# Four graph layers on one core: where GpSimd waits between the row gathers of the last attention layer

## The chip, the core and the metric

The kernel runs on one core of a Trainium2 chip. The metric is device microseconds of a plain (not profiled) execution. Three such executions of the kernel before took 5525.43, 5527.91 and 5542.02 us; the median is 5527.91 us. Engines are named PE (TensorE), PEld (its weight loads), DVE (VectorE), ACT (ScalarE), POOL (GpSimd) and SP (the queue that issues plain DMAs).

## The reference

A node table x of 3125 x 64 goes through four residual graph layers over the same 100,000 edges, sorted by destination: a GAT layer, a two-step SAGE layer, a layer that multiplies gathered rows by edge attributes, and a softmax attention with 8 heads, where the change is. Cut to what matters:

```
h = maximum(layernorm(x), 0)
src, dst = edges plus one self loop per node
z = (h @ W_att).reshape(n, 8, 64)
e = leaky_relu(a_src[src] + a_dst[dst], 0.2)         # a score per edge and head
e = exp(e - segment_max(e, dst)[dst])
alpha = e / (segment_sum(e, dst)[dst] + 1e-16)
out = segment_sum(alpha[:, :, None] * z[src], dst)   # then mean over heads, layer norm, feed-forward
```

## The kernel before

The four layers run one after the other. The changed loop is in `attend3`, the attention of the last layer (tiles with the prefix `l3_` in the program, `l_` in profile rows). What it does:

- The edges are cut into 782 tiles of 128 (`TILES`). For each tile POOL issues one indirect DMA, which gathers 128 rows of 73 floats (64 features, a one, 8 source scores) from `table3` into one of 320 places of the ring `rows` (`RING3`), at L1740. This is the loop `for t in range(TILES)` of the `gpsimd` block.
- 64 tiles are a part (`PART`), 13 parts in all (`NP`). A part's scores are made together: PE turns the gathered scores around (`turn_far`, L1898) once all its tiles have landed; DVE adds, takes running maxima and chains them over the tiles (`score`, L1759 to L1789, `join`, `settle`); ACT takes the exponentials (L1969).
- The sums go in 981 steps, each a pair of a tile and a window of 16 nodes, 4 steps to a group, 246 groups. For a group ACT copies the weights (`step_att`, L1981), DVE builds `hot` (L1845), PE multiplies (`sums`, L1934, two matmul records a step) and counts `sums_ready` up by one, DVE adds into `acc` (L1855). Places and windows are read at run time into registers (L194, TENSOR_LOAD, and FUSED_REGOPS, which work them out).
- Part p+1 is scored in the middle of part p: after the fifth group of a part (`SCORED` = 4) come `turn_far` and `score`, after the eighth `join`, after the eleventh `settle`. A part has 16 groups, the last part the rest.

The order of every engine is written out by hand; nothing is scheduled at run time, and the engines meet only at semaphores. POOL waits at two places in its loop. One is `landed` (L1739): before a tile it waits until the DMAs of the eight gathers just issued (a batch, `U` = 8) have landed. The other is `sums_ready` (L1737): before tiles t to t+7 go into the ring it waits until so many groups of sums are done that the old tiles in these places are certainly used up. The count that it waits for is (t + 7 - 320 + 199) // 4 + 1, that is (t - 114) // 4 + 1, where 199 is the number of windows less one. `RING3` (320), `REST` (2), `U` (8) and `PART` (64) are constants at the top.

Of the kernel before, what the change touches and what calls it, by code (L numbers as in the profile page):

```python
# [32 lines left out]
U = 8  # L33
# [23 lines left out]
REST = 2  # L57
# [20 lines left out]
PART = 64  # L78
NP = -(-TILES // PART)
RING3 = 320  # L80
# [1540 lines left out]
def part_tiles(p):  # L1621
    return min(PART, TILES - PART * p)


def attend3(nc, m):
# [6 lines left out]
    with ExitStack() as stack:  # L1632
# [41 lines left out]
        def landed(b):  # L1674

            return rows_in[b % RING], base[b % RING] + 16 * U * (b // RING) + 16 * min(U, TILES - U * b)
# [47 lines left out]
        @block.gpsimd  # L1724
        def _(pool):
            nc.gpsimd.memset(key_i[2][:, :], -1).then_inc(keys_blank, 1)
            def tile_firsts(p, landed):
                n = part_tiles(p)
                pool.indirect_dma_start(tile_first[0:n, p, :], None, m.node_values[:, :],
                                        bass.IndirectOffsetOnAxis(ap=m.first_tile[0:n, p:p + 1], axis=0)).then_inc(landed, 16)  # L1730
            tile_firsts(0, first_in)
            for t in range(TILES):
                if t == PART:
                    for p in range(1, NP):
                        tile_firsts(p, firsts_in)
                if t >= RING3 and t % 8 == 0:
                    pool.wait_ge(sums_ready, (t + 7 - RING3 + NW - 1) // STEPS + 1)  # L1737
                if t and t % (REST * U) == 0:
                    pool.wait_ge(*landed(t // U - 1))  # L1739
                pool.indirect_dma_start(rows[:, t % RING3, :], None, m.table3[:, :],  # L1740
                                        bass.IndirectOffsetOnAxis(ap=m.tile_src[:, t:t + 1], axis=0)
                                        ).then_inc(rows_in[t // U % RING], 16)
            pool.wait_ge(top_written, 16 * NP)
            for c in range(2 * J):
                pool.indirect_dma_start(found[:, c // J, c % J, :], None, m.reference[:, :],
                                        bass.IndirectOffsetOnAxis(ap=m.found_index[:, c // J, c % J:c % J + 1], axis=0)
                                        ).then_inc(found_in, 16)

        @block.vector
        def _(dve):  # L1750
# [61 lines left out]
            def settle(p):  # L1812

                n = part_tiles(p)
                N_ = slice(0, n)
                dve.wait_ge(back, p + 1)
                own(v.tensor_copy(first_last[N_, :, :], small_ps[N_, 4 * PART:4 * PART + 2 * H].rearrange("p (a h) -> p a h", a=2)))
                own(v.tensor_copy(ends[:, 0:1], ends[:, 2 * n:2 * n + 1]))
                if p:
                    _, values = nc.values_load_multi_w_load_instructions(  # L1820
                        m.start_step[0:1, p - 1:p], engines=[mybir.EngineType.DVE], min_val=0, max_val=KJ - 1,
                        skip_runtime_bounds_check_because="a tile's last step is under KJ - 1")
                    own(v.scalar_tensor_tensor(factor[:, bass.ds(values[0], 1)], small_ps[:, 4 * PART + 2 * H:4 * PART + 2 * H + 1],
                                               m.mask3[:, p:p + 1], m.unmask3[:, p:p + 1], ALU.mult, ALU.add))
                for a, inside in enumerate((in_first, in_last)):
                    own(v.tensor_tensor(near[N_, :, :], over(inside[N_, :].unsqueeze(1), (n, H, TILE)),
                                        over(first_last[N_, a, :].unsqueeze(2), (n, H, TILE)), ALU.add))
                    last = v.tensor_tensor(top[N_, :, :], near[N_, :, :], top[N_, :, :], ALU.max)
                    if a == 0:
                        own(last)  # L1830
                last.then_inc(top_ready, 1)
                dve.wait_ge(top_ready, p + 1)
                v.tensor_tensor(z[N_, :, :], z[N_, :, :], top[N_, :, :], ALU.subtract).then_inc(z_ready, 1)
# [508 lines left out]
```

## Time and profile before

| | |
|---|---|
| Plain executions | 5525.43, 5527.91, 5542.02 us |
| Profiled execution, first to last instruction (span) | 5821.8 us |
| Instructions | 59032 |
| PE, DVE, ACT, POOL busy in the span | 57%, 61%, 38%, 38% |
| Gathers of the third layer (L1143) | 782, 2796.6 to 3932.2 us |
| Gathers of the attention (L1740) | 782, 4076.3 to 5381.2 us |
| Steps of the attention (L1934) | 4206.5 to 5619.2 us |

The profiled execution is one execution recorded by the hardware. Its page gives no other time of it than the span; the span alone is 293.9 us longer than the median of the plain executions. All places in time below are microseconds from the span's start. A row "idle before <- X" says how long the engine stood still before that instruction and what ended the wait; "issue" is time for which no cause is recorded. Where such a cause names a DMA of another stage, the semaphore had been used by that DMA before.

### The profile page before, as it was taken

The page shows a single profiled execution, that of the slowest core. Times are in us where ns is not written, and L with a number is a line of the kernel's source. Part 1 is how long each engine was busy: PE and PEld are TensorE (multiplying, and loading weights), DVE is VectorE, ACT ScalarE, POOL GpSimd, SP SyncE. Part 2 cuts the span into 40 slices and gives each one's busy share as a digit, 9 for nine tenths or more (in the row PEclk, how much of TensorE's full clock was granted, in tenths as well). Part 3 has the DMA queues.
Part 4 walks back from the last instruction along what each step waited for, and adds up shares of the span by engine and source line. Part 5 has one row for each costly group of instructions (what it writes and reads, how often), then busy time and mean ns, then how long its engine had stood idle before and what let it go on. Part 6 is the DMA issues. An engine that isn't in the chain of part 4 may idle for free. (4 is left out here: it accounts for less than half of the span.)

```text
span 5821.8 us, 59032 instructions
## 1 busy us (share of the span) xinstructions
PE 3339.7 (57%) x14332; PEld 2165.0 (37%) x14332; DVE 3534.5 (61%) x6569; ACT 2187.4 (38%) x3989; POOL 2214.4 (38%) x2086
## 2 busy tenths in 40 slices
PE   5666679999999999789034332333000443433565
PEld 3555534444444444456032332333000443333452
DVE  6999989999999999310134332333211664545676
ACT  4999967878788887200000000000000111111210
POOL 0000023333333333000666777772777056666200
PEclk8999989999999999899556555555555555555556
DMA  2555544444444443787321422212111012111011
GB/s 74 163 162 162 162 131 114 119 111 111 119 109 116 116 115 97 155 187 157 57 45 38 92 47 43 50 34 22 35 28 33 9 33 36 31 36 30 5 36 35
DMA packets 546254, 474.35 MB, mean 81 GB/s; under 512 B 185774, under 2 KB 439737, under 8 KB 545086
## 3 DMA queue, kind: packets, MB, share of 16 engines
q1 hardware_dynamic: 493723, 416.13, 28.5%
q0 software_dynamic: 52288, 55.34, 5.9%
q8 instruction: 109, 1.79, 0.1%
q14 instruction: 134, 1.09, 0.1%
HBM read 351.39 MB, written 119.84 MB: 81 GB/s over the span
## 5 line engine op out<-in xcount | busy, mean ns | idle before, releaser
L815 PE MATMUL l_sum_ps<-arena,sums 125*65 125x500 f32 (+1 forms) x2600 | 1144.6, 578 | 9.9 <-ACT arena L776 4.8
L1740 POOL DMA_INDIRECT l_rows<-table,tile_src x782 | 768.9, 983 | 521.1 <-issue 232.6
L1143 POOL DMA_INDIRECT l_rows<-hidden_rows,tile_src x782 | 794.9, 1017 | 341.8 <-issue 231.5
L694 POOL COPY arena<-arena 125x750 f32<-125x750 f32 (+1 forms) x400 | 538.9, 1351 | 894.6 <-PE l_count_ps L804 864.9
L760 ACT ACTIVATE arena<-arena,far_left 125x750 f32<-125x750 f32 (+1 forms) x800 | 713.3, 939 | 285.7 <-DVE arena L713 285.7
L713 DVE SCALAR_TENSOR_TENSOR arena<-arena,far_past 125x750 f32<-125x750 f32 (+1 forms) x800 | 807.1, 1055 | 16.1 <-DMA arena<-score_rows 16.1
L1204 PE MATMUL l_sum_ps<-l_rows,l_hot 128*125 x1612 | 360.1, 414 | 768.6 <-issue 651.9
L724 DVE SCALAR_TENSOR_TENSOR arena<-arena,l_count_ps 125x750 f32<-125x750 f32 (+1 forms) x800 | 739.4, 970 | 100.5 <-ACT arena L765 52.0
L1934 PE MATMUL l_sum_ps<-l_rows,l_hot 128*128 x1962 | 483.6, 424 | 439.3 <-issue 268.9
L1170 DVE TENSOR_TENSOR sums<-sums,l_sum_ps 125x64 f32 x806 | 178.6, 222 | 777.9 <-DMA arena<-counts 485.6
L1204 PEld LDWEIGHTS l_sum_ps<-l_rows,l_hot 128*125 128x125 f32 x1612 | 341.3, 322 | 787.7 <-issue 786.9
L1934 PEld LDWEIGHTS l_sum_ps<-l_rows,l_hot 128*128 128x128 f32 x1962 | 437.8, 327 | 483.9 <-issue 481.3
L1855 DVE SCALAR_TENSOR_TENSOR acc<-acc,l_factor,l_sum_ps 128x65 f32 x981 | 276.4, 282 | 542.4 <-DMA found_index<-found_rows 319.6
L765 ACT ACTIVATE arena<-arena 125x1500 f32<-125x1500 f32 (+1 forms) x400 | 596.1, 1491 | 0.0
L507 PE MATMUL l0tab_count_ps<-l0tab_pair_hot,l0tab_src_hot 125*125 125x325 bf16 x2592 | 427.3, 307 | 224.9 <-issue 199.3
L815 PEld LDWEIGHTS l_sum_ps<-arena,sums 125*65 125x65 f32 x2600 | 353.0, 141 | 541.7 <-issue 541.4
L804 PEld LDWEIGHTS l_count_ps<-ident,arena 125*125 125x125 f32 x2500 | 314.4, 192 | 392.3 <-issue 342.9
L1243 ACT ACTIVATE l_end_dense_sb<-l_end_ps_t 128x500 f32<-128x500 f32 (+1 forms) x7 | 3.7, 542 | 1210.0 <-PE l_end_ps_t L1229 1209.9
L507 PEld LDWEIGHTS l0tab_count_ps<-l0tab_pair_hot,l0tab_src_hot 125*125 125x125 bf16 x2592 | 329.7, 137 | 322.6 <-issue 309.2
L804 PE MATMUL l_count_ps<-ident,arena 125*125 125x125 f32 x2500 | 371.4, 287 | 130.3 <-POOL arena L694 55.2
L471 DVE TENSOR_SCALAR l0tab_pair_hot<-code_iota,fine_pair_code 125x650 bf16<-125x650 f16 x1296 | 418.3, 392 | 1.0 <-PE l0tab_count_ps L507 1.0
L486 ACT ACTIVATE arena<-node_iota,fine_src_code 125x125 f32<-125x125 f32 x1296 | 405.9, 384 | 0.0
(440 smaller groups left out, 3021.8 us busy)
## 6 DMA issues: line engine op xcount, KB each, us to landing
arena<-counts SPq DMA_DIRECT2D x300, 328.1 KB
counts<-arena SPq DMA_DIRECT2D x324, 284.4 KB
arena<-counts SPq DMA_DIRECT2D x17, 2843.8 KB
arena<-counts SPq DMA_DIRECT2D x100, 382.8 KB
l_attr<-edge_attr_in SPq DMA_DIRECT2D x97, 256.0 KB
arena<-score_rows SPq DMA_DIRECT2D x24, 732.4 KB
l_rows<-hidden_rows,tile_src POOLq DMA_INDIRECT x782
l_rows<-table,tile_src POOLq DMA_INDIRECT x782
```

Source lines behind the costliest of these rows:

```text
L507: last = nc.tensor.matmul(self.ps[b][0:P, c, 0:CW // 2], self.src_hot[b][:, t, :], self.pair_hot[b][:, t, c * (CW // 2):(c + 1) * (CW // 2 ...
L694: g.tensor_copy(laid[k % 2][:, 0:n * P].rearrange("p (b v d) -> p b v d", b=n, d=D), raw[k % RAWS][:, 0:n * P].rearrange("p (v b d) -> p b ...
L713: last = v.scalar_tensor_tensor(scores(k)[:, i, :], rows[:, 1, i, :], m.far_past[:, w, h:h + 1], rows[:, 0, i, :], ALU.add, ALU.max)
L724: last = v.scalar_tensor_tensor(here, here, LOWEST, over(count_ps[0:P, c, 0:hi - lo].unsqueeze(1), (P, PAIR, hi - lo)), ALU.max, ALU.mult)
L760: last = nc.scalar.activation(here, here, ACT.Relu, scale=-1.0, bias=m.far_left[:, w, h:h + 1])
L765: nc.scalar.activation(scores(k), scores(k), ACT.Exp, scale=-1.0).then_inc(raised, 1)
L804: last = nc.tensor.transpose(count_ps[0:P, i // per, o:o + P], laid[k % 2][:, i * P:(i + 1) * P], m.ident[0:P, 0:P])
L815: last = nc.tensor.matmul(sum_ps[0:F + 1, c, 0:hi - lo], h_one[:, w, :], z[k % ZS][:, lo:hi], start=(w == 0), stop=(w == W - 1))
L1143: pool.indirect_dma_start(rows[:, b % RING, t, :], None, m.hidden_rows[:, :], bass.IndirectOffsetOnAxis(ap=m.tile_src[:, k:k + 1], axis=0) ...
L1204: last = nc.tensor.matmul(sum_ps[r % 4][0:P, j * F:(j + 1) * F], hot[r % 4][:, j, :], flat[:, bass.ds(place, 1), :].rearrange("p a f -> p ...
L1740: pool.indirect_dma_start(rows[:, t % RING3, :], None, m.table3[:, :], bass.IndirectOffsetOnAxis(ap=m.tile_src[:, t:t + 1], axis=0)).then_ ...
L1934: last = nc.tensor.matmul(sum_ps[g % 4][:, i * (F + 1):(i + 1) * (F + 1)], hot[g % 3][:, i, :, :].rearrange("p h j -> p (h j)"), rows[:, b ...
```

## The change

Both conditions of POOL's loop are set by t, the number of the tile.

```diff
@@ -1733,9 +1733,9 @@
                 if t == PART:
                     for p in range(1, NP):
                         tile_firsts(p, firsts_in)
-                if t >= RING3 and t % 8 == 0:
+                if t >= 2 * PART and t % 8 == 0:
                     pool.wait_ge(sums_ready, (t + 7 - RING3 + NW - 1) // STEPS + 1)
-                if t and t % (REST * U) == 0:
+                if t and t % (U if t >= 2 * PART else REST * U) == 0:
                     pool.wait_ge(*landed(t // U - 1))
```

The wait for sums is made from tile 128 on (before: from tile 320, where it is needed to keep the ring intact). The wait for the last eight gathers is made before each eighth tile from 128 on (before: each sixteenth throughout). Up to tile 127, nothing changes. No other engine's instructions and no transfer is changed.

The first place is POOL's order from tile 112 on. `rows_in11` and the like are the semaphores of `landed` (one of twelve for each batch), `shared24` is `sums_ready`; "x15" is fifteen gathers in a row with no wait. In the program before:

```order
L1740 DMA l3_rows<-table3,tile_src 128x73 [waits rows_in1]
L1740 DMA l3_rows<-table3,tile_src 128x73 x15
L1740 DMA l3_rows<-table3,tile_src 128x73 [waits rows_in3]
L1740 DMA l3_rows<-table3,tile_src 128x73 x15
L1740 DMA l3_rows<-table3,tile_src 128x73 [waits rows_in5]
L1740 DMA l3_rows<-table3,tile_src 128x73 x15
```

The same stretch of POOL's order in the changed program:

```order
L1740 DMA l3_rows<-table3,tile_src 128x73 [waits rows_in1]
L1740 DMA l3_rows<-table3,tile_src 128x73 x15
L1740 DMA l3_rows<-table3,tile_src 128x73 [waits rows_in3,shared24]
L1740 DMA l3_rows<-table3,tile_src 128x73 x7
L1740 DMA l3_rows<-table3,tile_src 128x73 [waits rows_in4,shared24]
L1740 DMA l3_rows<-table3,tile_src 128x73 x7
L1740 DMA l3_rows<-table3,tile_src 128x73 [waits rows_in5,shared24]
L1740 DMA l3_rows<-table3,tile_src 128x73 x7
```

The first two rows (tiles 112 to 127) are the same; from tile 128 on a stop stands before each eighth gather, and each also waits for sums.

The second place is POOL's order from tile 320 on, as a piece of the difference between the two programs (- before, + changed):

```order
 L1740 DMA l3_rows<-table3,tile_src 128x73 [waits rows_in3,shared24]
 L1740 DMA l3_rows<-table3,tile_src 128x73 x7
-L1740 DMA l3_rows<-table3,tile_src 128x73 [waits shared24]
+L1740 DMA l3_rows<-table3,tile_src 128x73 [waits rows_in4,shared24]
 L1740 DMA l3_rows<-table3,tile_src 128x73 x7
 L1740 DMA l3_rows<-table3,tile_src 128x73 [waits rows_in5,shared24]
 L1740 DMA l3_rows<-table3,tile_src 128x73 x7
```

Here the stops stay where they were, each eighth gather; every second one, which waited for sums alone, now waits for the landing too.

## Rows read from the trace of the kernel before

**Rows 1.** The page: span, and POOL's busy tenths in 40 slices.
```profile
span 5821.8 us, 59032 instructions
...
POOL 0000023333333333000666777772777056666200
```

**Rows 2.** Busy us (x instructions) by stretch; last PE clock, DMA share, GB/s.
```profile
300.00:900.00 600.00, 411.34 (x2235) 283.27 (x2236) 568.38 (x1226) 519.43 (x1188) 46.49 (x34) 0.97 0.51 152
900.00:2400.00 1500.00, 1367.23 (x5052) 626.10 (x5051) 1388.89 (x1536) 1183.08 (x1123) 522.82 (x400) 0.97 0.44 112
2400.00:2700.00 300.00, 268.06 (x1251) 170.88 (x1250) 32.93 (x64) 11.33 (x28) 0.00 (x0) 0.95 0.95 198
2796.00:3933.00 1137.00, 362.25 (x1550) 327.02 (x1550) 353.84 (x990) 0.00 (x0) 795.19 (x784) 0.52 0.26 51
4076.00:4523.00 447.00, 35.84 (x160) 31.11 (x160) 80.19 (x155) 23.16 (x84) 319.45 (x333) 0.50 0.19 32
4523.00:4675.00 152.00, 81.81 (x351) 73.47 (x352) 114.89 (x291) 35.52 (x188) 0.94 (x1) 0.50 0.05 12
4675.00:5383.00 708.00, 265.06 (x1119) 232.92 (x1119) 385.68 (x951) 114.95 (x477) 461.03 (x462) 0.50 0.19 33
```

**Rows 3.** The gathers of L1740: min/median/max ns, and their idle time by cause.
```profile
L1740 POOL DMA_INDIRECT l_rows<-table,tile_src x782: 946/952/1953, 4076.3 to 5381.2; - x196
...
  issue: 232.6, 728
  PE l_sum_ps L1934: 209.9, 18
```

**Rows 4.** Timeline of POOL: gathers after a stop; start, length, idle before.
```profile
4264.20 0.95 POOL L1740 DMA_INDIRECT l_rows<-table,tile_src  x1 [1.73 <-DMA l_rows<-table,tile_src]
4265.46 0.95 POOL L1740 DMA_INDIRECT l_rows<-table,tile_src  x1 [0.30 <-issue]
...
4675.74 0.95 POOL L1740 DMA_INDIRECT l_rows<-table,tile_src  x1 [151.80 <-PE l_sum_ps L1934]
...
4791.43 0.95 POOL L1740 DMA_INDIRECT l_rows<-table,tile_src  x1 [3.84 <-PE l_sum_ps L1934]
...
4804.01 0.95 POOL L1740 DMA_INDIRECT l_rows<-table,tile_src  x1 [2.28 <-DMA l_rows<-table,tile_src]
```

**Rows 5.** Timeline of PE: the starts of parts 1, 2, 3, 5 and 11 (L1898).
```profile
4264.08 1.90 PE L1898 MATMUL l_far_ps<-ident,l_rows 128*64 128x128 f32 x8 [10.16 <-DMA l_rows<-table,tile_src]
...
4557.44 1.91 PE L1898 MATMUL l_far_ps<-ident,l_rows 128*64 128x128 f32 x8
...
4617.38 1.91 PE L1898 MATMUL l_far_ps<-ident,l_rows 128*64 128x128 f32 x8
...
4776.61 1.90 PE L1898 MATMUL l_far_ps<-ident,l_rows 128*64 128x128 f32 x8 [17.04 <-DMA l_rows<-table,tile_src]
4788.11 0.58 PE L1906 MATMUL l_small_ps<-ident,l_pack 64*8 64x64 f32 x4 [9.60 <-DVE l_pack L1789]
4789.20 4.03 PE L1934 MATMUL l_sum_ps<-l_rows,l_hot 128*128 x16 [0.51 <-DVE l_hot L1845]
...
5356.15 1.90 PE L1898 MATMUL l_far_ps<-ident,l_rows 128*64 128x128 f32 x8 [9.53 <-DMA l_rows<-table,tile_src]
```

**Rows 6.** ACT's register work at L1981, min/median/max ns: 4208 to 4298, then 4541 to 4560.
```profile
L1981 ACTq FUSED_REGOPS  x51: 6/700/1396, 4208.2 to 4296.3; - x51
...
L1981 ACTq FUSED_REGOPS  x40: 64/64/64, 4541.2 to 4549.2; - x40
```

**Rows 7.** Timeline of DVE: one group while POOL stands still.
```profile
4551.84 0.69 DVE L1845 TENSOR_TENSOR l_hot<-l_here,l_step_att 128x512 f32<-128x512 f32 x1
4552.51 1.56 DVE L1855 SCALAR_TENSOR_TENSOR acc<-acc,l_factor,l_sum_ps 128x65 f32 x4
4553.98 0.42 DVE L1841 TENSOR_TENSOR l_here<-rel,window_iota 128x256 f32<-128x256 f32 x1
```

**Rows 8.** The gathers of the third layer (L1143): min/median/max ns.
```profile
L1143 POOL DMA_INDIRECT l_rows<-hidden_rows,tile_src x782: 946/952/1926, 2796.6 to 3932.2; - x196
```

## The prediction

> **What bounds the kernel now.** I read the page first, for the span and for the engine that is busy throughout the changed stage. The reader is to see two blocks of POOL work late in the span, the third layer's gathers and the attention's [rows 1]. Then I read busy time by stretch. From 300 to 2700 us an engine or the DMAs are busy nine tenths of the time: DVE 568 of 600 us, DVE 1389 and PE 1367 of 1500 us, the DMAs 0.95 [rows 2]. In the two gather stretches none of PE, DVE and ACT is: DVE has 354 of 1137 us, and 80 of 447 us at the attention's start [rows 2]. What runs steadily there is POOL. One gather takes 0.952 us in the median [rows 3] and is followed by 0.30 us before the next [rows 4], so 1.252 us a tile; 782 of them are 979 us, most of the 1307 us from 4076 to 5383.
>
> What stands between 979 and 1307 is in POOL's timeline [rows 4] and in the summary by cause [rows 3]: short stops of 1.73 to 2.28 us for landings, stops for sums (209.9 us in all), and among these one of 151.80 us, at tile 320, until 4675. That one tells the story of the recorded execution. While POOL streamed 320 gathers without a wait for sums, the other engines hardly moved: part 1's scores were turned at 4264, part 2's only at 4557, after POOL had stopped [rows 5]. With POOL still, a part then took 4617.38 - 4557.44 = 59.9 us, for 16 groups of which each costs DVE 0.69 + 1.56 us [rows 7].
>
> So two readings are open. Either the streaming starves the consumers, and the change, which brakes POOL from tile 128 on, cures it; or the starving is of the recording. The next view decides for me: ACT's register work. The same FUSED_REGOPS, which works on registers alone, takes 64 ns when POOL stands still and 700 ns in the median while it streams [rows 6]. An operation without a memory access, slowed eleven times, looks like an engine that must wait to write its record. And the total agrees: the span is 5821.8 us [rows 1], the plain median 5527.9, so 293.9 us are not there when nobody records. The stretches before 2700 us have no room for them. The gather stretches have: the third layer 1137 - 979 = 158 us (782 gathers of the same 952 ns [rows 8]), and the attention 1307 - 979 - 16 (13 more gathers at L1729, at the same pace) - 71 (48 landing stops at 1.77 - 0.30 = 1.47 us) - 28 (8 stops for sums at 3.84 - 0.30 = 3.54 us, explained below) = 213 us. The 293.9 us are 79% of these 371 us. At most 21% of the stalls are left in a plain execution, and less if anything lies around the span there.
>
> The Trainium skill (Runtime: NRT & Kernel Launch, section on the preamble and postamble) says that a profile's total exceeds the reported time by some 6.2 us whatever the kernel. By that rule the stalls would be the kernel's own. The trace disagrees here, with 293.9 us, and I follow the measurement; the rule's result is rival A.
>
> In a plain execution POOL then paces the attention: it needs 64 x 1.252 + 4 x 1.47 + 3.54 = 89.5 us a part, the consumers 59.9 us. Every microsecond by which POOL gets later moves the last full part, and from there the consumers' fixed work runs to the end (5356 to the last step).
>
> **The change, part by part.**
>
> *The landing stops.* From tile 128 on, the odd multiples of eight get one: (776 - 136) / 16 + 1 = 41 new stops. One in four of them (tile 64p + 8) falls on a stop for sums, which is longer and covers it: 11 of them, p = 2 to 12. Of the 30 others all lie before tile 768, so all delay part 11. The price of one: in the free stretch a stop is 1.73 us where 0.30 would stand, net about 1.45; among working consumers it is 2.28, net 1.98 [rows 4]. I take 1.6, nearer the free stretch, since the plain consumers are idle a third of the time: 30 x 1.6 = 48 us. Nothing lies under it that POOL could do; behind the waiting gather are queued all later gathers, and PE's next turn_far waits for these (17.04 us before part 5 [rows 5]). Bounds: 30 x 0 = 0 if POOL has slack that I don't see, and 30 x 3.54 = 106 us if each stop costs as much as the longest common one.
>
> The Trainium skill (DMA: Bandwidth & Descriptors, section on the anatomy of a DMA) puts a DMA's fixed cost at about 2.0 us, mostly the receipt of the last byte, and this speaks against a wait for what was just issued. By its fit 37 KB cost 2.09 us, net of the usual gap 1.79, and the term would be 54 us instead of 48.
>
> *The wait for sums from tile 128.* POOL waits at tile t for (t - 114) // 4 + 1 groups. At t = 64p + 8 that is 16p - 26, one group more than are done when part p-1's turn_far starts. The trace shows the price at part 5: turn_far at 4776.61, score, first group after it from 4789.20, POOL released at 4791.43 after 3.84 us [rows 4, 5]. This stop exists before for p = 5 to 12; new are p = 2, 3, 4: 3 x 3.54 = 11 us. At the next stops two more groups each are asked for per 8 x 1.252 = 10.0 us, and DVE makes a group in 2.25 us [rows 7]; 59.9 us a part against 80 leave them covered. The first one, tile 128, asks for 4 groups, done long before. Bounds: 0, and 24 stops x 3.54 = 85 us if the consumers lag at each.
>
> *The relief.* What is left of the starving in plain runs should go. Most of it was paid back by the stop of 151.8 us: at most 0.21 x 151.5 = 32 us, at least 0. I take half, 16.
>
> *What is not touched.* The ring, the transfers' size and number, the order on PE, DVE, ACT and SP. PE's clock is 0.50 of full (the 1.2 GHz level) through the whole stage [rows 2], too little work before and after.
>
> Sum: 48 + 11 - 16 = +43 us. On the recorded axis another sum holds, since there the starving counts in full: from 4264 the steady pace (5356.15 - 4776.61) / 6 = 96.6 us a part, up to 96.6 + 3 x 1.98 = 102.5 with the new stops, would bring part 11 to 4264 + 966 to 1025 = 5230 to 5289, against 5356: the recorded span gets shorter by 67 to 126 us, to about 5726, while the plain time gets longer. Plain: 5527.9 + 43 = 5571 us (+0.8%).
>
> **The rivals.**
>
> A. *The starving is real.* For it: the stalls are in the trace, and the cure fits them. Against: 64 ns against 700 ns, and the 293.9 us. Place: tiles 128 to 320. It decides if more than about two fifths of the stop of 151.8 us (59 of 151.5) exists in plain runs. In full it gives what the recorded axis gives, -96 us: 5432 us, faster.
>
> B. *No change to be told.* The landing without a recorder comes sooner than 1.73 us, say net 1.0 (30 us), and relief is the full 32: 30 + 11 - 32 = +9, 5537 us. For it: no trace shows a plain landing. Against: a stop must outlast the last transfer's flight.
>
> C. *The wait for sums holds at every stop.* If plain consumers are slower than I read, the 24 stops before tile 320 cost up to 85 us: 48 + 85 - 16 = +117, 5645 us. Against: 59.9 us a part while POOL is silent.
>
> **How the numbers follow.** Forecast 58%, own range 5551 (44 + 11 - 32 = +23) to 5598 (59 + 11 = +70); A 20%, B 15%, C 7%. A measurement of this kernel can tell about 0.3% (17 us) from no change. Faster is A, 20%; within 0.3% is B, 15%; slower is the forecast and C, 65%. The range reaches from A's nearer side, a relief half real, 5470, to 5625 between forecast and C; left out are the rest of A (some 14%) and of C (4%).
>
> **What would show it.** In the changed profile POOL has no stop above 20 us between 4076 and 5383; its idle time for sums falls from 209.9 us below 80; there are 89 landing places instead of 48, and the stops at tiles 64p + 24, + 40, + 56 are 1.7 to 2.3 us. Part 2 is turned near 4365 instead of 4557. The span falls to 5650 to 5760. If the plain time falls too, the step that failed is the one that put the stalls down to the recording; if the plain time stays, the price of a stop. If the span doesn't fall, the starving comes back in each run of eight.

## The result, and the profile after

The changed kernel takes 5595.65 us (median of 4 executions, 5594.18 to 5597.14); the kernel before took 5526.67 us beside it (4 executions, 5523.14 to 5542.02). The ratio is 1.012, 95% interval 1.0108 to 1.0132: slower by 69 us where +43 was forecast.

The page of the changed kernel, against [rows 1]:

```profile
span 5592.4 us, 59085 instructions
...
POOL 0000023333333333300077777774666666666300
```

The third layer's gathers are the digits 77777774, the attention's the 666666666 behind them: even, without the empty slice of [rows 1], where POOL stood still for 151.80 us. The span fell from 5821.8 to 5592.4 us, much further than the forecast 5650 to 5760.

Busy us by stretch (columns as in [rows 2]), two of the same stretches and the time after:

```profile
2796.00:3933.00 1137.00, 420.74 (x1856) 381.60 (x1856) 409.88 (x1116) 7.56 (x15) 819.57 (x785) 0.52 0.26 52
4077.00:4524.00 447.00, 152.34 (x656) 136.04 (x656) 220.12 (x543) 67.50 (x339) 289.59 (x292) 0.50 0.18 34
4524.00:5384.00 860.00, 372.55 (x1576) 332.57 (x1576) 489.62 (x1242) 154.02 (x693) 449.71 (x456) 0.50 0.14 26
```

From 4077 to 4524 us DVE now does 220 us of work, where [rows 2] has 80 in the same place. That alone tells little, since the attention began 106 us earlier in this recording (3970.7 for 4076.3). And the third layer, which the change doesn't touch, is further on too: in the same 1137 us PE has done 1856 instructions where [rows 2] has 1550. PE's granted clock is as before.

The gathers of the attention (answers to [rows 3]) and of the third layer (to [rows 8]); the columns are min/median/max ns, first and last start:

```profile
L1740 POOL DMA_INDIRECT l_rows<-table,tile_src x782: 946/952/1922, 3970.7 to 5185.8; - x196
...
  issue: 212.5, 694
  DMA l_rows<-table,tile_src: 156.1, 69
  PE l_sum_ps L1934: 61.7, 19
...
L1143 POOL DMA_INDIRECT l_rows<-hidden_rows,tile_src x782: 947/952/1936, 2795.9 to 3849.1; - x196
```

The third layer ends at 3849.1 instead of 3932.2, 83 us earlier where nothing was changed: POOL is idle before its gathers for 238.2 us and no longer for 341.8. ACT's register work tells the same, with nothing over 175 ns ([rows 6] had a median of 700 ns while POOL streamed):

```profile
L1981 ACTq FUSED_REGOPS  x1377: 42/64/175, 4084.9 to 5354.7; - x197
```

POOL's timeline among the first tiles of part 3 (tiles 200, 208, 209 and 216; answers to [rows 4]):

```profile
4276.06 0.95 POOL L1740 DMA_INDIRECT l_rows<-table,tile_src  x1 [3.85 <-PE l_sum_ps L1934]
...
4288.26 0.95 POOL L1740 DMA_INDIRECT l_rows<-table,tile_src  x1 [2.24 <-DMA l_rows<-table,tile_src]
4289.57 1.90 POOL L1740 DMA_INDIRECT l_rows<-table,tile_src  x1 [0.36 <-issue]
...
4301.19 0.95 POOL L1740 DMA_INDIRECT l_rows<-table,tile_src  x1 [2.19 <-DMA l_rows<-table,tile_src]
```

And PE's, the starts of parts 1, 2, 3 and 11 (answers to [rows 5]):

```profile
4160.41 1.89 PE L1898 MATMUL l_far_ps<-ident,l_rows 128*64 128x128 f32 x8 [63.26 <-DMA l_rows<-table,tile_src]
...
4261.24 1.90 PE L1898 MATMUL l_far_ps<-ident,l_rows 128*64 128x128 f32 x8 [42.34 <-DMA l_rows<-table,tile_src]
...
4361.38 1.90 PE L1898 MATMUL l_far_ps<-ident,l_rows 128*64 128x128 f32 x8 [41.83 <-DMA l_rows<-table,tile_src]
...
5164.52 1.89 PE L1898 MATMUL l_far_ps<-ident,l_rows 128*64 128x128 f32 x8 [40.99 <-DMA l_rows<-table,tile_src]
```

The parts come every 100.4 us ((5164.52 - 4160.41) / 10). Before part 1 PE stands still for 63.26 us and before each of the ten that follow for 40.5 to 43.0 us, and waits for rows. POOL paces the stage, and the price of each stop is paid in full.

### The profile page after: what moved, and what is told of

Read it like the earlier page. It is cut to its first block and busy times, and to the rows that moved or that the text cites. A ratio compares the mean times of both kernels' runs of the same rounds, so it can differ in the third digit from the quotient of the medians.

```text
span 5592.4 us, 59085 instructions
## 1 busy us (share of the span) xinstructions
PE 3330.3 (60%) x14332; PEld 2163.3 (39%) x14332; DVE 3537.9 (63%) x6569; ACT 2178.9 (39%) x3989; POOL 2241.4 (40%) x2086
## 3 DMA queue, kind: packets, MB, share of 16 engines
q8 instruction: 109, 1.79, 0.1%
## 5 line engine op out<-in xcount | busy, mean ns | idle before, releaser
L1740 POOL DMA_INDIRECT l_rows<-table,tile_src x782 | 769.9, 984 | 430.3 <-issue 212.5
L1143 POOL DMA_INDIRECT l_rows<-hidden_rows,tile_src x782 | 816.1, 1044 | 238.2 <-issue 238.2
L1160 DVE TENSOR_TENSOR l_rows<-l_rows,l_attr 128x512 f32<-128x512 f32 x98 | 69.1, 705 | 543.6 <-DMA l_rows<-hidden_rows,tile_src 543.6
L1898 PE MATMUL l_far_ps<-ident,l_rows 128*64 128x128 f32 (+1 forms) x104 | 24.6, 417 | 609.9 <-DMA l_rows<-table,tile_src 609.9
```

The costliest lines, as they stand in the source:

```text
L1143: pool.indirect_dma_start(rows[:, b % RING, t, :], None, m.hidden_rows[:, :], bass.IndirectOffsetOnAxis(ap=m.tile_src[:, k:k + 1], axis=0) ...
```

## The experiments

Each kernel is timed against the kernel before on the same chip; the diffs are against the changed kernel unless said otherwise.

### Was the starving the kernel's or the recording's?

The kernel before, unchanged, recorded a second time.

> The kernel before, unchanged, recorded a second time. If the starving of the first recording (ACT's FUSED_REGOPS at 700 ns, POOL's stop of 151.8 us at tile 320, a span 294 us above the plain median) belongs to the recording, it need not come again: then the span is 5520 to 5540 us, the register operations stay at 64 ns, no stop of POOL is above 10 us, and part 2's turn_far comes about 90 us after part 1's. If it belongs to this order of waits, the span is again near 5820 us with the stop at tile 320.

It took 5529.24 us, and its span was 5527.5 us. Its gathers, their idle time by cause, and ACT's register work:

```profile
L1740 POOL DMA_INDIRECT l_rows<-table,tile_src x782: 946/952/1936, 3972.6 to 5118.7; - x196
...
  issue: 225.5, 728
  DMA l_rows<-table,tile_src: 93.8, 44
  PE l_sum_ps L1934: 35.9, 10
...
L1981 ACTq FUSED_REGOPS  x1377: 42/64/175, 4086.7 to 5287.4; - x197
```

Idle time for sums is 35.9 us where the first recording has 209.9 [rows 3], and POOL's stop at tile 320 is 2.29 us long, not 151.80 [rows 4]. Its parts 1, 2 and 11 start here:

```profile
4162.35 1.89 PE L1898 MATMUL l_far_ps<-ident,l_rows 128*64 128x128 f32 x8 [63.38 <-DMA l_rows<-table,tile_src]
...
4253.08 1.90 PE L1898 MATMUL l_far_ps<-ident,l_rows 128*64 128x128 f32 x8 [32.43 <-DMA l_rows<-table,tile_src]
...
5097.41 1.90 PE L1898 MATMUL l_far_ps<-ident,l_rows 128*64 128x128 f32 x8 [36.58 <-DMA l_rows<-table,tile_src]
```

From 4077 to 4524 us this recording has 222.23 us of DVE work, as much as the changed kernel: what the two pages differ in there is not the change's doing. So the stalls of the first recording are not in the kernel, and this recording is the right "before". From part 1 to part 11 it needs 935.1 us and the changed kernel 1004.1: the whole 69 us lie there. The page's lines on L1740 (busy, mean ns | idle before) balance it, first of this recording:

```profile
L1740 POOL DMA_INDIRECT l_rows<-table,tile_src x782 | 776.0, 992 | 355.3 <-issue 225.5
```

and of the changed kernel:

```profile
L1740 POOL DMA_INDIRECT l_rows<-table,tile_src x782 | 769.9, 984 | 430.3 <-issue 212.5
```

Idle +75.0, busy -6.1: +68.9 us.

### The two halves of the change, each alone

Only the wait for sums is moved to tile 128 (sums_only):

```diff
-                if t and t % (U if t >= 2 * PART else REST * U) == 0:
+                if t and t % (REST * U) == 0:
```

> The wait for sums from tile 128, the landing waits as before (each sixteenth). Theory (each landing stop costs its idle time, the wait for sums costs 3.54 us at tiles 136, 200, 264 and nothing elsewhere): +11 us on the kernel before, 5537 us, up to +17 if the landing stops at 128 to 319 grow from 1.77 to 2.25 us because they stand beside a second wait. Rival (holding POOL back behind the sums is what costs, at each of 24 stops): +40 to +69 us, nearly the whole loss.

5542.66 us (11 executions) against 5530.01, ratio 1.002 (1.001 to 1.003): +12.7 us. Besides the three new stops for sums, the landing stops that were there already are longer from tile 128 on, here at tile 192:

```profile
4254.26 0.95 POOL L1740 DMA_INDIRECT l_rows<-table,tile_src  x1 [2.24 <-DMA l_rows<-table,tile_src]
```

Only the landing waits are doubled (land_only):

```diff
-                if t >= 2 * PART and t % 8 == 0:
+                if t >= RING3 and t % 8 == 0:
```

> The landing wait each eighth gather from tile 128, the wait for sums from tile 320 as before. Theory: 41 new stops less the 8 under an old stop for sums = 33 at 1.95 us (idle 2.25 less 0.30) where a sums wait stands beside, 1.47 where it doesn't (tiles 136 to 312: 12 stops): 21 x 1.95 + 12 x 1.47 = +59 us, 5585 us. If the second wait has no part in the 2.25, 33 x 1.95 = +64. Rival (the sums cost): near 0 to +29 us.

5583.91 us (5 executions) against 5530.01, ratio 1.0092 (1.0077 to 1.0107): +53.9 us. The halves add up to 66.6 of the 69 us. In POOL's timeline of land_only (tiles 240, 248, and then 336, 352) the price of a landing stop is seen to change at tile 320:

```profile
4316.55 0.95 POOL L1740 DMA_INDIRECT l_rows<-table,tile_src  x1 [1.82 <-DMA l_rows<-table,tile_src]
4328.11 0.95 POOL L1740 DMA_INDIRECT l_rows<-table,tile_src  x1 [1.82 <-DMA l_rows<-table,tile_src]
...
4462.20 0.95 POOL L1740 DMA_INDIRECT l_rows<-table,tile_src  x1 [2.23 <-DMA l_rows<-table,tile_src]
...
4487.84 1.46 POOL L1740 DMA_INDIRECT l_rows<-table,tile_src  x1 [2.19 <-DMA l_rows<-table,tile_src]
```

The consumers (PE, DVE and ACT) work at both places. What differs is that from tile 320 on the same gather also waits for sums: a stop with one semaphore is about 1.77 us, one with two about 2.25, though the second had long been reached. The two halves show it at one place too: at tile 192 the stop is 1.73 us here, with one semaphore, and 2.24 in sums_only, with two.

### The two waits on different gathers

```diff
-                if t >= 2 * PART and t % 8 == 0:
-                    pool.wait_ge(sums_ready, (t + 7 - RING3 + NW - 1) // STEPS + 1)
+                if t + 1 >= 2 * PART and (t + 1) % 8 == 0:
+                    pool.wait_ge(sums_ready, (t + 8 - RING3 + NW - 1) // STEPS + 1)
```

> The changed kernel with its waits for sums made one gather earlier (before tile t - 1 for the tiles from t on), so that no gather has two waits. Theory: a stop for a landing costs 1.77 us of idle time when it is the gather's only wait and 2.25 us when a wait for sums stands beside it on the same gather, whatever the other engines do; apart, the 71 landing stops from tile 128 that no stop for sums covers fall to 1.77: -0.48 x 71 = -34 us on the changed kernel, 5562 us. Rival (the landing takes longer because the consumers are at work): no change, 5596 us.

5603.94 us (4 executions) against 5528.22, ratio 1.014 (1.0122 to 1.0158). It is 8 us slower than the changed kernel, where a gain of 34 was expected: a miss. POOL's timeline at tiles 135, 136 and 144, 145:

```profile
4177.88 0.95 POOL L1740 DMA_INDIRECT l_rows<-table,tile_src  x1 [5.10 <-PE l_sum_ps L1934]
4180.57 0.95 POOL L1740 DMA_INDIRECT l_rows<-table,tile_src  x1 [1.74 <-DMA l_rows<-table,tile_src]
...
4192.60 0.95 POOL L1740 DMA_INDIRECT l_rows<-table,tile_src  x1 [1.79 <-DMA l_rows<-table,tile_src]
4193.85 1.98 POOL L1740 DMA_INDIRECT l_rows<-table,tile_src  x1 [0.30 <-issue]
...
L1740 POOL DMA_INDIRECT l_rows<-table,tile_src x782 | 781.5, 999 | 426.1 <-issue 206.6
```

The landing stops did fall to 1.77 us, which is worth 0.48 each. But POOL comes to the stop for sums one gather earlier and is released no earlier, so that it lasts 1.25 us longer (5.10 for 3.85), and the landing stop behind it is no longer covered (1.74 - 0.30). Per part 8 landing stops at 1.77 and one of 5.10 are 19.3 us, against 7 at 2.25 and one of 3.85, 19.6: nothing is gained, and POOL's idle time on L1740 is 4.2 us less in all. The other 11.6 us are busy time: the mean gather took 999 ns instead of 984. The median is 952 in both; single gathers take up to 1.98 us. The long ones are not scattered by chance. All 109 that last over 1.0 us overlap an instruction of DVE, and of the 360 gathers that overlap none, the longest takes 961 ns. Moving a stop moves the gathers against DVE's work: in each of eleven parts one of them now meets L1778, which none does in the changed kernel. The rows of the next run show such a meeting.

### Waiting for the batch before last

```diff
-                    pool.wait_ge(*landed(t // U - 1))
+                    pool.wait_ge(*landed(t // U - 2))
```

> The changed kernel with one thing different: at each stop POOL waits for the batch before the last one (landed(t // U - 2)), so for transfers issued at least 10 us earlier. The number and place of the waits are the same. Theory (the price is the flight of the last transfer, 1.5 to 2 us a stop): all landing stops go, the 89 of the changed kernel, and only the 11 stops for sums stay: against the changed kernel -(78 x about 1.9) = -148 us, 5448 us, which is 79 us under the kernel before. Rival (a wait costs by itself, an instruction more for POOL's queue): 5580 to 5596 us as the changed kernel. Rival (the pauses feed the other engines, so taking them away starves them): above 5527 us.

5468.9 us (4 executions), ratio 0.9884 (0.9866 to 0.9902). All 82 landing places from tile 128 on stay, and none has a stop for its landing: what they wait for was issued at least 8 gathers before. POOL's timeline at tiles 192, 193 and 200:

```profile
4236.98 0.95 POOL L1740 DMA_INDIRECT l_rows<-table,tile_src  x1 [0.30 <-issue]
4238.24 0.95 POOL L1740 DMA_INDIRECT l_rows<-table,tile_src  x1 [0.30 <-DMA l_rows<-table,tile_src]
...
4253.16 0.95 POOL L1740 DMA_INDIRECT l_rows<-table,tile_src  x1 [5.10 <-PE l_sum_ps L1934]
...
L1740 POOL DMA_INDIRECT l_rows<-table,tile_src x782 | 781.0, 999 | 291.8 <-issue 220.9
```

It missed its forecast by 21 us for two reasons that the rows show. The eleven stops for sums grew by 1.25 us each, from 3.85 to 5.10 or from 4.04 to 5.29, 14 us in all: they end when the first group after turn_far ends, and POOL now comes earlier. And the gathers' busy time grew by 11.1 us. Against the changed kernel that is 430.3 - 291.8 - 11.1 = 127.4 us less; measured 126.8.

What makes single gathers long is seen at tiles 132 and 133 of this run, first DVE's rows, then POOL's:

```profile
4153.14 1.22 DVE L1778 SCALAR_TENSOR_TENSOR l_z<-l_z 64x1024 f32<-64x1024 f32 x1
4154.39 1.87 DVE L1779 TENSOR_TENSOR l_far_ps<-l_z,l_raw 64x1024 f32<-64x1024 f32 x1
4153.59 1.59 POOL L1740 DMA_INDIRECT l_rows<-table,tile_src  x1 [0.30 <-issue]
4155.49 1.61 POOL L1740 DMA_INDIRECT l_rows<-table,tile_src  x1 [0.30 <-issue]
```

Each gather begins while a DVE instruction runs and ends 0.82 to 0.84 us after that instruction (4155.18 after 4154.36, 4157.10 after 4156.26). Of the 107 gathers over 1.0 us in this run 94 end so, after L1778, L1779, L1826, L1841, L1845 or L1762; L1855, L1783 and L1784 run as well when gathers begin, and no gather ends like that after them. No run moved a DVE instruction alone, so that the tie is read from the times and not tested.

The same edit on the kernel before (older_b):

> The kernel before with one edit: each sixteen gathers POOL waits for the batch before last instead of the last one. Theory (a landing stop costs 1.47 to 1.95 us, and nothing once what it waits for is 8 gathers old; the sums stop at tiles 64p + 8 grows by what the landing stop at 64p spared, from 3.85 to 5.1): per part 80.1 for 64 paces, 3.3 of long gathers, from tile 320 on 4.8 for the sums stop: eight parts lose 6.3 each against before, the four before them 7 each: 5527 - 50 - 28 = 5449 us. Between it and the kernel measured above stand only the eight sums stops, 8 x 4.8 = 38 us at most, less some longer gathers: 5426 + 25 to 38. Rival (a satisfied second wait on an instruction costs its 0.48 us too): 8 x 3 x 0.48 = 12 us above, 5461 us.

5462.14 us (4 executions, 5457.9 to 5469.61) against 5529.9, ratio 0.9882 (0.9867 to 0.9897). Its first estimate, 5449, missed by 13 us and its second, 5451 to 5464, holds. The time is also the rival's, but its reason is not: no satisfied wait shows over 0.31 us. What I had left out is again the gathers' busy time, 784.0 for 776.0 us; idle time fell by 77.9, as expected.

### When the first group after turn_far comes later

```diff
-SCORED, JOINED, SETTLED = 4, 7, 10
+SCORED, JOINED, SETTLED = 5, 7, 10
```

> The changed kernel with SCORED = 5: turn_far and score come after a part's sixth group instead of its fifth. Theory: the stop at tile 64p + 8 asks for one group more than are done when turn_far starts; with the sixth group ahead of it the stop for sums goes and the landing stop of 2.25 us comes out from under it: 11 x (3.85 - 2.25) = -18 us on the changed kernel, 5578 us. Rival (the stop comes from the consumers' pace, not from this order): no change.

5584.55 us (4 executions) against 5528.22, ratio 1.0107 (1.009 to 1.0124). With one more group done before a part is scored, POOL's wait at tile 64p + 8 is met, and the landing stop that it had covered shows in its place (tile 200):

```profile
4270.27 0.95 POOL L1740 DMA_INDIRECT l_rows<-table,tile_src  x1 [2.27 <-DMA l_rows<-table,tile_src]
```

18 us were expected and 11 measured between the medians; the two recorded executions, 5594.18 and 5576.5 us, are 17.7 apart, and L1740's idle time fell by 18.7. So the stop for sums is made by the order of PE's work, as [rows 4, 5] let one read.

### The landing waits doubled from tile 448 only

```diff
-                if t and t % (U if t >= 2 * PART else REST * U) == 0:
+                if t and t % (U if t >= 7 * PART else REST * U) == 0:
```

> The changed kernel with the landing wait each eighth gather only from tile 448 on (each sixteenth before it), the waits for sums from tile 128 as in the changed kernel. Theory (each new landing stop costs 1.95 us, wherever it is): it drops 20 of the 41 new stops, of which 5 (tiles 136, 200, 264, 328, 392) were covered by a stop for sums: 15 x 1.95 = -29 us on the changed kernel, 5566 us. Rival (the first stretch, tiles 128 to 320, is what matters): at least -50 us.

5567.58 us (6 executions), ratio 1.0077 (1.0062 to 1.0092). That is 28.1 us less than the changed kernel, 29 were expected, for 15 uncovered stops left out before tile 448. The 15 uncovered ones from there on cost as much: this run is 39.4 us above the kernel before and sums_only, which has none of the new landing stops, 12.7, so 26.7. POOL has no slack, early or late in the stage.

### Both stops gone

The kernel before, with the wait for the batch before last and SCORED = 5.

> The kernel before (waits for sums from tile 320, landing waits each sixteenth) with two edits: the landing waited for is that of the batch before the last one, and SCORED = 5. Theory: POOL then never stops; 782 gathers at the pace of 88.5 us a part of the run with the older batch, less its eleven stops of 5.1 us (net 4.8 each): 5469 - 53 = 5416 us. Rival (POOL streaming without a stop starves the others): above 5469 us.

5425.69 us (median of 6), ratio 0.9816 (0.98 to 0.9833). One of the executions took 15763.43 us and is left out of the ratio, so it was measured again:

> The kernel that waits for the landing of the batch before last, with the scores begun one group later (SCORED = 5), measured once more, because one of its six executions took 15763.43 us. Theory (that execution was a disturbance of the chip): about 5426 us in every execution, ratio 0.982. Rival (the kernel itself stalls now and then): another execution of many thousand us among these.

5427.94 us (5 executions, 5423.29 to 5434.63) against 5529.9, ratio 0.982 (0.9806 to 0.9833); the long one did not come again. The page's line on L1740, in both recordings with the same busy and idle sums, here the first:

```profile
L1740 POOL DMA_INDIRECT l_rows<-table,tile_src x782 | 790.7, 1011 | 238.3 <-issue 230.4
```

The forecast was 5416 us; the 10 us above it are the gathers' busy time again, 790.7 us where the run it was reckoned from has 781.0. 133 gathers are over 1.0 us here, 79 in the changed kernel. 238.3 us are 782 x 0.305: only the gap between two gathers is left, and no stop. The sum 1029.0 is 102.3 us less than in the kernel before, measured 102.5 and 102.0.

## Why the prediction was right, step by step, and where not

*What bounds the kernel: right.* POOL paces the attention. The forecast 89.5 us a part has a stop for sums in it, so it is to be held against the parts from tile 320 on: the second recording has 94.5 us there (parts 4 to 11 start from 4435.60 to 5097.41). Of the 5 us that were missing, 1.9 are the second wait on four landing stops, 4 x 0.48, and 2.3 are gathers longer than the median; I had priced neither. From part 1 to part 2, with no stop for sums, it is 90.7 us (4253.08 - 4162.35), where the same terms give 86.0.

*The accounting: right in what it concluded, wrong in its books.* I gave the 293.9 us to the recording, because register work took 700 ns [rows 6] and the total did not agree. The second recording has 64 ns and no stalls. "At most 21% are left" holds for the stalls: none are. But the sum behind it was off. The two stretches shrank from 1137 to 1052 us and from 1307 to 1147, by 245 us; 49 of the 293.9 lay outside them, and 126 of the 371 us that I took for stalls are still there. In the third layer 69 of these are gathers longer than the median (813.9 us busy for 782 x 0.952 = 744.5), with no stop among them. It did no harm, since the relief was bounded by nothing at its lower end. Every later recording is free of them as well. Whether the recorder or something else disturbed that one execution, the runs don't tell; "it must wait to write its record" was only argued.

The Trainium skill (Runtime: NRT & Kernel Launch, section on the preamble and postamble) has a profile's total some 6.2 us above the reported time. The span here counts from the first to the last instruction and need not be the total that the Trainium skill means. It is 1.7 us below its own reported time in the second recording (5527.5 and 5529.24), and in the first 293.9 us above the plain median: neither shows a gap of 6.2 us.

*The landing stops: counted right, priced too low.* The 30 uncovered new stops were forecast at 1.6 us net, 48 us. They cost 2.25 - 0.30 = 1.95, so 58.5 us. The step that failed is "among working consumers it is 2.28": the consumers have nothing to do with it, land_only shows 1.8 us beside them. What makes 2.25 of 1.77 is the second semaphore on the same gather, and the change gives it to every stop. With that, 12 landing stops that were there already (tiles 128 to 304, each sixteenth) became dearer by 0.48, 5.8 us that my sum had not.

The Trainium skill (DMA: Bandwidth & Descriptors, section on the anatomy of a DMA) gives about 2.0 us fixed, from which I had estimated a net 1.79 a stop. It is above the 1.47 of a stop with one wait and below the 1.95 of one with two.

*The wait for sums: right.* Three new stops for sums of 3.85 us, at tiles 136, 200 and 264; at the other new places two are longer than 2.5 (2.91 at tile 152, 3.57 at tile 600), but nothing repeats there: 3 x 3.55 = 10.6 us, forecast 11. The idle time for sums is 61.7 us, forecast below 80.

*The relief: wrong.* I took 16 us for what might be left of the starving. There was none to relieve.

The sum with measured terms: 58.5 + 5.8 + 10.6 = 74.9 (the idle time rose by 75.0), less 6.1 for the gathers, which were a little shorter on the mean: 68.8, measured 69. Of the 26 us between forecast and result, 16 are the relief and 16.3 the stops (10.5 and 5.8), less the 6.1 of the gathers. That the 5.8 I had not seen and the 6.1 I had not seen cancel is luck. The result lies near the upper end of the own range, 5598, and that end was the sum with no relief and 1.98 us a stop, which is what ran.

*The recorded axis: wrong.* The forecast of 5650 to 5760 for the span took the starving of the first recording as a property of every recording. It was one of a single one, and of the 229 us by which the span fell, the third layer alone brought 83. Part 2 was turned at 4261 and not near 4365; the stage began 106 us earlier. From start to part 2 the forecast is 4365 - 4076 = 289 us and the trace 4261.24 - 3970.7 = 291.

*The rivals.* A fell with the second recording: a plain kernel has no starving to cure. B needed a landing below 1.73 us; the stops are as long in undisturbed recordings. C would have shown as idle time for sums at each stop; there are 61.7 us in 19 stops, 11 of which are those at 64p + 8.

## What to carry to other kernels

When a profile's span is far above the plain time, record the same kernel again before explaining any stall in it; a register instruction that took eleven times its length was the sign here. On an engine that paces its stage, a wait for what was just issued costs the rest of its flight every time, and a wait for the batch before it costs nothing and still bounds how many transfers are out. Before a stop is moved, see which stop it covers: it may uncover one as long as itself.

## What the runs showed of the hardware

- The landing of a gather of 128 rows x 292 bytes, waited for by the next gather, stops POOL for 1.77 us with one semaphore and 2.25 us with two, also where the second is long reached (1.73 and 2.24 us at tile 192 of land_only and sums_only); with the wait on a batch 8 gathers old the stop is 0.30 us, the usual gap.
- A gather takes 952 ns in the median in every run, but the mean rises as the stops go: 984 ns in the changed kernel (430.3 us idle), 992 before (355.3), 999 (291.8), 1011 without any stop (238.3). It is not the stops alone: with the two waits on different gathers it is 999 beside 426.1 us idle. Single gathers take up to 1.98 us. In the changed kernel 348 gathers overlap no DVE instruction and the longest of them takes 961 ns; in the fastest kernel it is 273 and 961 ns. All longer ones overlap one (79 and 133 are over 1.0 us), and most end 0.82 to 0.84 us after it ends. This gave back 14.7 of the 117 us of idle time that the fastest kernel saved.
- One recorded execution of an unchanged kernel had a span 293.9 us above the plain median, with register instructions at 700 instead of 64 ns while gathers streamed; no other of the recordings shown here has them.
